# Where a graph kernel puts its running group states: scattered to each node's row as they finish, or stored densely and gathered by node at the end

## The reference

```python
w_m = (efeat @ W_msg + b_msg).reshape(E, in_f, -1)
w_a = (efeat @ W_attn + b_attn).reshape(E, in_f, -1)
h_src = feat[src][:, :, None]
e1 = w_m * h_src
e2 = w_a * h_src
seg_max = jax.ops.segment_max(e2, dst, num_segments=N)
ex = jnp.exp(e2 - seg_max[dst])
denom = jax.ops.segment_sum(ex, dst, num_segments=N)
attn = ex / denom[dst]
ft = jax.ops.segment_sum(e1 * attn, dst, num_segments=N)
return ft.sum(axis=1)
```

## Time and profile before

| | us |
|---|---|
| median of 3 runs | 6419.38 (6419.01 to 6424.5) |
| the profiled execution's time | 6420.29 |
| its span | 6418.6 |
| DVE busy in the span | 5261.2 (82%) |
| POOL busy | 4903.2 (76%) |
| PE busy | 4765.4 (74%) |
| ACT busy | 2628.9 (41%) |

### The profile page before, as it was taken

One profiled execution on the slowest core, in us unless ns is written; L12 is line 12 of the kernel. 1 busy time (PEld: TensorE's weight loads), 2 busy tenths in 40 slices (PEclk: granted clock), 3 DMA queues, 4 the chain that ended last, 5 costly groups with the idle time before them and its releaser, 6 DMA issues. The chain is left out here.

```text
span 6418.6 us, 70875 instructions
## 1 busy us (share of the span) xinstructions
PE 4765.4 (74%) x18115; PEld 2257.7 (35%) x18115; DVE 5261.2 (82%) x8583; ACT 2628.9 (41%) x4866; POOL 4903.2 (76%) x4618
## 2 busy tenths in 40 slices
PE   1277777777777777775888888888888888888881
PEld 1133333333333333342333333333333333333330
DVE  5366666666666666667999999999999999999996
ACT  1122222222222222213555555555555555555553
POOL 6688888888888888855777777777777777777772
PEclk6588888888889898897889899989989889889895
DMA  4122222222222222210111111111111111111102
GB/s 123 50 68 72 68 68 69 68 68 72 63 54 54 54 54 54 53 39 13 16 17 16 16 16 16 16 16 17 16 16 16 16 16 16 16 16 16 16 15 105
DMA packets 386589, 255.80 MB, mean 40 GB/s; under 512 B 243117, under 2 KB 334678, under 8 KB 386305
## 3 DMA queue, kind: packets, MB, share of 16 engines
q0 software_dynamic: 226240, 167.32, 12.5%
q1 hardware_dynamic: 160318, 88.15, 4.6%
HBM read 186.95 MB, written 141.36 MB: 51 GB/s over the span
## 5 line engine op out<-in xcount | busy, mean ns | idle before, releaser
L587 POOL DMA_INDIRECT bg<-btab,mt x1600 | 2109.2, 1318 | 489.6 <-issue 464.3
L697 PE MATMUL pagg<-ohh,stt 125*128 125x512 bf16 x4800 | 1847.0, 421 | 743.6 <-DVE ohh L627 743.6
L947 POOL DMA_INDIRECT xg<-x1tab,edge x1920 | 1917.2, 999 | 550.0 <-issue 549.7
L1029 PE MATMUL ps<-work,ident 128*128 128x512 f32 x3840 | 2006.4, 647 | 0.2 <-DVE work L1117 0.2
L698 PE MATMUL pagg<-ohh,stt 125*128 125x270 bf16 x4800 | 1454.7, 303 | 0.0
L1078 DVE TENSOR_TENSOR work<-pw,xg 128x1024 f32<-128x1024 f32 x960 | 1125.8, 1214 | 56.8 <-DMA xg<-x1tab,edge 25.8
L1029 PEld LDWEIGHTS ps<-work,ident 128*128 128x128 f32 x3840 | 817.5, 213 | 748.2 <-issue 656.1
L697 PEld LDWEIGHTS pagg<-ohh,stt 125*128 125x128 bf16 x4800 | 510.6, 106 | 1496.5 <-DVE ohh L627 822.0
L678 ACT COPY ohx<-ohl 125x1024 bf16<-125x1024 bf16 x200 | 208.8, 1044 | 1971.7 <-DVE ohl L617 1971.7
L610 DVE TENSOR_TENSOR bg<-bg,e 125x1024 f32<-125x1024 f32 x200 | 245.1, 1225 | 839.6 <-DMA bg<-btab,mt 839.6
L988 ACT ACTIVATE work<-work,mt 128x256 f32<-128x256 f32 x1920 | 793.1, 498 | 3.5 <-DVE work L1078 3.3
(11 more groups left out here) (232 smaller groups left out, 4247.6 us busy)
## 6 DMA issues: line engine op xcount, KB each, us to landing
xg<-x1tab,edge POOLq DMA_INDIRECT x1920, 2.4
bg<-btab,mt POOLq DMA_INDIRECT x1600, 3.5
rtab<-zrow SPq DMA_DIRECT2D x56, 384.0 KB, 3.9
tab<-rtab SPq DMA_DIRECT2D x7, 2048.0 KB, 8.4
etab<-joined SPq DMA_DIRECT2D x200, 66.4 KB
e<-in_edge_attr_dram SPq DMA_DIRECT2D x200, 62.5 KB
e<-in_edge_attr_dram SPq DMA_DIRECT2D x200, 31.2 KB
mt<-meta SPq DMA_DIRECT2D x240, 6.0 KB, 1.8
```

The costliest lines, as they stand in the source:

```text
L587: g.indirect_dma_start(bg[:, h, i, :], None, btab, bass.IndirectOffsetOnAxis(ap=mt[:, h, 0, i:i + 1], axis=0)).then_inc(gathered[h], 16)
L697: pe.matmul(pagg[:, 0, :], w, ohh[:, h, i, 0:CUT], start=False, stop=False, skip_group_check=True)
L947: g.indirect_dma_start(xg[:, b % 4, i, :], None, x1tab, bass.IndirectOffsetOnAxis(ap=edge[:, b, i, D:D + 1], axis=0)).then_inc(x_in[b % 4] ...
L1029: pe.matmul(ps[:, b % 2, :], ident[:, :], work[:, b % 4, i, :, :, :].rearrange("p i a o -> p (i a o)"), start=i == 0, stop=False)
```

## The change

- `rtab` is gone. Two dense tables take its place, `smax` (one row of 256 floats for each group) and `ssum` (512 floats), with two fixed rows behind them, `EMPTY` and `NEUTRAL`.
- In the second layer's loop SP stores every tile's whole `state` with two DMAs (128 x 2 KB and 128 x 1 KB), then loads the `mt` of 8 tiles on. POOL's scatter and its wait are gone. DVE's write into a state buffer waits for both stores of 8 tiles earlier.
- In setup DVE works out for each node the number of its last group (7 small operations); SP writes it to `lasttab` and reads it back into `lasti` (3 DMAs). `meta1` shrinks from 12 to 10 words a group.
- The 56 + 2 filling DMAs of the first layer are replaced by 4 of one row each.
- In the merge the tails are read from the last group of each partition by SP, the heads with two indirect gathers on POOL.
- At the end 56 indirect gathers on POOL (7 blocks x 8, each 128 rows of 2 KB) replace SP's 7 loads, and DVE takes over POOL's multiplication.

```diff
@@ setup, vector
+                v.memset(pado[:, :], EMPTY).then_inc(last_step, 1)
+                v.tensor_scalar(final, first[:, 1:], float(E), None, ALU.is_ge).then_inc(last_step, 1)
...
+                v.tensor_scalar(lasto[:, :], final, float(EMPTY), None, ALU.add).then_inc(last_step, 1)
@@ setup, sync
+                sp.wait_ge(last_step, 7)
+                sp.dma_start(lasttab[0:N].rearrange("(p t) -> p t", p=P), lasto[:, :]).then_inc(last_out, 16)
+                sp.dma_start(lasttab[N:NPAD].rearrange("(p t) -> p t", t=9), pado[:, :]).then_inc(last_out, 16)
+                sp.wait_ge(last_out, 32)
+                sp.dma_start(lasti[:, :, :], lasttab.rearrange("(b p l) -> p b l", p=128, l=LO)).then_inc(last_in, 16)
@@ first layer, sync
-                    sp.dma_start(view[:, bass.ds(t * 3 * C, 3 * C)], zrow[:, :]).then_inc(table_cleared, 16)
@@ second layer, sync
+                def store(n, q):
+                    sp.wait_ge(st_done, n + 1)
+                    sp.dma_start(ssum[0:GP * NT, :].rearrange("(p t) c -> p (t c)", p=GP)[:, bass.ds(n * 2 * C, 2 * C)],
+                                 state[:, q, C:3 * C]).then_inc(stored[q], 16)
+                    sp.dma_start(smax[0:GP * NT, :].rearrange("(p t) c -> p (t c)", p=GP)[:, bass.ds(n * C, C)],
+                                 state[:, q, 0:C]).then_inc(stored[q], 16)
...
-                        sp.wait_ge(scattered[q], 16 * (t + 1))
+                        store(U * t + q, q)
                         load(U * t + q + U, q)
@@ second layer, gpsimd
-                    if at := tile(t, q, -2):
-                        n, b, r = at
-                        g.wait_ge(st_done, n + 1)
-                        g.nop(nofuse=True)
-                        g.indirect_dma_start(rtab, bass.IndirectOffsetOnAxis(ap=mt[:, b, 1:2], axis=0),
-                                             state[:, b, :], None,
-                                             bounds_check=ROWS - 1, oob_is_err=False).then_inc(scattered[b], 16)
@@ second layer, vector
-                    wait(v, scattered[b], 16 * r)
+                    wait(v, stored[b], 32 * r)
@@ merge, gpsimd
+                at = bass.IndirectOffsetOnAxis(ap=hrow[:, 0:1], axis=0)
+                g.indirect_dma_start(ht[:, 0, 0:C], None, smax, at).then_inc(head_in, 16)
+                g.indirect_dma_start(ht[:, 0, C:3 * C], None, ssum, at).then_inc(head_in, 16)
@@ end, gpsimd
                 for b in range(NB):
-                    s = tab[:, b % 3, :, 0, :]
-                    g.wait_ge(guessed, b + 1)
-                    g.tensor_tensor(s, s, inv[:, b % 2, :, :], ALU.mult).then_inc(off_by, 1)
+                    if b >= 3:
+                        g.wait_ge(f_step, 4 * (b - 2))
+                    for l in range(LO):
+                        g.indirect_dma_start(tab[:, b % 3, l * D:(l + 1) * D, :, :].rearrange("p i a o -> p (i a o)"), None,
+                                             ssum,
+                                             bass.IndirectOffsetOnAxis(ap=lasti[:, b, l:l + 1], axis=0)).then_inc(row_in[b], 16)
@@ end, vector
                     v.tensor_tensor(t, t, inv[:, b % 2, :, :], ALU.mult).then_inc(f_step, 1)
-                    v.wait_ge(off_by, b + 1)
+                    v.tensor_tensor(s, s, inv[:, b % 2, :, :], ALU.mult).then_inc(f_step, 1)
```

More of the change, by code:

```diff
@@ L55 @@
 U = 8
-MW = 12
+MW = 10
 KS = 99
+EMPTY, NEUTRAL = GP * NT, GP * NT + 1
+ROWS = GP * NT + 2
+SKIP = ROWS
 assert GP * NT * J >= E + (J - 1) * N and NT % U == 0
@@ L117, in gnn @@
         ends = sb("ends", [GP, 8])
+        hrow = sb("hrow", [GP, 1], I32)
+        lasti = sb("lasti", [128, NB, LO], I32)
         consts_made = sem("consts_made")
@@ L337, in _ @@
                                             op0=ALU.mult, op1=ALU.add))
-                deg, num, run, has = (ngf[:, i, :] for i in range(4))
+                deg, num, run, has, final, lastg = (ngf[:, i, :] for i in range(6))
                 link(v.tensor_tensor(deg, first[:, 1:], first[:, 0:TN], ALU.subtract))
@@ L561, in _ @@
                 sp.wait_ge(rows_made, 4)
-                sp.dma_start(rtab[HEAD:HEAD + 128, :], hrow[:, :]).then_inc(table_cleared, 16)
-                sp.dma_start(rtab[TAIL:TAIL + 128, :], hrow[:, :]).then_inc(table_cleared, 16)
-                per = NPAD // 128
-                view = rtab[0:NPAD, :].rearrange("(p r) c -> p (r c)", p=128)
-                with sp.Fori(0, per) as t:
-                    next_pair(t)
-                    sp.dma_start(view[:, bass.ds(t * 3 * C, 3 * C)], zrow[:, :]).then_inc(table_cleared, 16)
-                with sp.Fori(per, NBLK // 2 - 1) as t:
+                for r in range(2):
+                    sp.dma_start(smax[EMPTY + r:EMPTY + r + 1, :], fixed[:, r, 0:C]).then_inc(table_cleared, 16)
+                    sp.dma_start(ssum[EMPTY + r:EMPTY + r + 1, :], fixed[:, r, C:3 * C]).then_inc(table_cleared, 16)
+                with sp.Fori(0, NBLK // 2 - 1) as t:
                     next_pair(t)
@@ L575, in _ @@
                     sp.wait_ge(join_out[h], 16 * (NBLK // 2 + 1))
-                sp.wait_ge(table_cleared, 16 * (per + 2))
+                sp.wait_ge(table_cleared, 64)
             @block.gpsimd
@@ L851, in gnn @@
             x_in = [sem(f"l1_x_in{q}") for q in range(4)]
-            scattered = [sem(f"l1_scattered{q}") for q in range(U)]
+            stored = [sem(f"l1_stored{q}") for q in range(U)]
             primed = sem("l1_primed")
@@ L910, in _ @@
                     for q in range(U):
-                        sp.wait_ge(scattered[q], 16 * (t + 1))
-                        sp.nop(nofuse=True)
+                        store(U * t + q, q)
                         load(U * t + q + U, q)
+                for q in range(U):
+                    store(NT - U + q, q)
+                for q in range(U):
+                    sp.wait_ge(stored[q], 32 * (NT // U))
             @block.gpsimd
@@ L955, in body @@
                                              bass.IndirectOffsetOnAxis(ap=mt[:, b, 0:1], axis=0)).then_inc(edge_in[b % 4], 16)
-                rounds(g, body, 5, 2)
-                for q in range(U):
-                    g.wait_ge(scattered[q], 16 * (NT // U))
+                rounds(g, body, 5, 0)
             @block.scalar
@@ L1102, in maxima @@
                     wait(v, corr_done, n)
-                    v.scalar_tensor_tensor(out=gap[:, :], in0=state[:, (b - 1) % U, 0:C], scalar=word(b, 2),
+                    v.scalar_tensor_tensor(out=gap[:, :], in0=state[:, (b - 1) % U, 0:C], scalar=word(b, 1),
                                            in1=state[:, b, 0:C], op0=ALU.add, op1=ALU.subtract).then_inc(gap_done, 1)
@@ L1215, in _ @@
                 v.tensor_tensor(rowf[:, 1:2], ends[:, 1:2], ends[:, 2:3], ALU.not_equal).then_inc(step, 1)
-                v.tensor_scalar(rowf[:, 2:4], ends[:, 0:2], -float(SKIP), None, ALU.add).then_inc(step, 1)
+                v.tensor_scalar(rowf[:, 2:3], ends[:, 3:4], -float(SKIP), None, ALU.add)
+                v.tensor_scalar(rowf[:, 3:4], iota_p[:, 1:2], -float(SKIP), None, ALU.add).then_inc(step, 1)
                 v.wait_ge(step, 5)
```

99 lines of the change are left out of this document (55 added, 44 removed).

## The result

The changed kernel takes 6465.16 us (4 runs, 6464.75 to 6469.23) against 6419.19 beside it (4 runs, 6416.78 to 6424.5): ratio 1.0072, 95% interval 1.0054 to 1.0089. It is slower, by 46 us (0.7%) where 113 were forecast. The profiled execution has a span of 6463.1, 44.5 more than the 6418.6 of before.

| stretch | before | after | difference | forecast |
|---|---|---|---|---|
| to the first maximum | 2968.5 | 2966.8 | -1.7 | -1 |
| loop, first to last maximum | 3293.1 | 3321.8 | +28.7 | +96 |
| last maximum to the first read of the table | 61.7 | 56.0 | -5.7 | +1 |
| first read to L1366 (L1336 before) | 83.8 | 107.0 | +23.2 | +17 |
| the layer norm behind it | 11.5 | 11.5 | 0 | 0 |

The account below looks back on a forecast made before the run. The prediction took the loop to be bound by DVE and POOL together, both full and coupled through PE. Loop +96, setup -1, merge +1 and end +17 gave +113 us, 6532 by the median; 8-in-10 range 6420 to 6575.

Parts of the forecast that it names:

- steps 1 and 2: Loop: without the scatter POOL needs 12.65 us a tile, DVE's wait for PE goes; POOL runs ahead until ACT's copy.
- Step 3, the place: Loop: POOL's two tensor operations move from under L1078 to under the last L1117, L1089 and L1090.
- Step 3, the price: Loop: collision priced by the second tile's 14.23 us, three stretched DVE operations, less 0.05 for the scatter: 14.18 a tile.
- The loop's term: Second layer's loop: 239 tiles at 14.18 us instead of 13.78, +96 us, with a range of +75 to +115.
- The single stretch: Rival, loop: only one DVE operation stretches, 13.73 us a tile, -12, with the end 6424; chance 0.10.
- The first rival: Loop: POOL's pair stays under L1078 or ahead of it, 13.51 us a tile, -64, total 6372; chance 0.16.
- The end: End of kernel: POOL's gathers replace SP's loads and DVE takes over POOL's multiplication; +17 us, between +10 and +26.
- nothing disturbs: End, lower case: DVE's blocks of 10.7 us run without POOL's gathers being held up, +10 us.
- a gather each: End, upper case: one gather gets through in each of three DVE operations, a block takes 13.5 us, +26.
- Between loop and end: Merge: two gathers of 1.28 us in place of two loads, +1 us.
- First layer, setup, stores: Outside the loop's collision: removing first-layer gathers is worth 0, setup -1 us, SP's stores cost 0.
- The full lock: Rival, loop: each of POOL's two operations costs DVE its whole 0.45 us, +62 more, 6594; chance 0.04.

Follow-up runs that it names:

- e4: Kernel after, with POOL's pair of tensor operations held until DVE's `gap` of the tile is done: 6470.9 us (one run).
- e1: Kernel after, with POOL's pair of tensor operations held until DVE's `carry_on` of that tile is done: 6412.5 us, ratio 0.9996 to the kernel before.
- e5: Kernel after, with 1/denominator and the first product of the end in PSUM, leaving DVE's tensor-tensor operations one SBUF input each: 6458.8 us.
- e3: Kernel after, with each tile's state stored twice, the second time into tables nobody reads: 6468.4 us (one run).
- e10: Kernel after, with POOL's pair held until `carry_on` and its order swapped, end operands in PSUM, and a wait making a gap in DVE's products: 6397.8 us.
- e6: Kernel after, with POOL's pair held until `carry_on` and the end's operands in PSUM: 6406.9 us.

## Why the prediction was right, and where it was wrong

- **What bounds the kernel, and steps 1 and 2**: right. PE's wait for the pair went (517.2 to 38.1 us), the edges' four take 4.61, POOL moved up until ACT's copy stopped it, in 230 tiles.
- **Step 3, the place**: right. The pair begins under the last product (0.02 us after its start) and goes on under L1115 and L1116, where the prediction had put it.
- **Step 3, the price**: this is the step that failed. "I price them by the tile that shows this collision: 14.23 us" took three stretched operations from the earlier trace rows. After the change the pair stretches two: 13.51 + 2 x 0.22 = 13.95 by the prediction's own figures, 13.90 measured. The tile taken for the price was one in which POOL ran straight from a gather into L933 (0.01 us between them). Step 2 had POOL wait for ACT ahead of that operation in each tile, and in the traces a pair that comes after a wait never stretches the operation that already runs. So the price of step 3 came from a state that step 2 had ruled out. The kernel before has no pair that comes after a wait with such an operation running, so its trace could not tell the price; e4 and the kernel after could. The third stretch was 0.23 x 239 = 55 us of the miss, the difference of 13.95 and 13.90 the other 12. The tile had no scatter either (the first starts at 3001.15 us), so the 0.05 that the prediction took off for it was not there to be taken off; this went the right way by luck. The loop's term was +96 and is +28.7, 67 us less. The total missed by 67 too, because the end (6 us more than forecast) and the stretch ahead of it (7 less) cancel, which is luck.
- **The single stretch**, the rival at 6424, was 41 us too low, where the forecast was 67 too high. The measured time lies between the two, where the prediction had put no case, though its wide range took it in.
- **The first rival** (POOL stays clear) did not come by itself. e1 made it by hand and found its tile, 13.51, but not its mean: 13.68, for PE's clock.
- **The end**: +23.2 against +17, inside 10 to 26. The middle between "nothing disturbs" and "a gather each" was too kind. The upper case is what the later blocks show: three of eight gathers are held, and the block is 13.0 us for its 13.5, since the held ones start every 2.2 us or so and the others every 1.25. DVE began 17.9 us after the first gather, against 18.5. e5 shows that DVE's second SBUF input is the cause.
- **Between loop and end**: -5.7 against +1. The last scatter before the barrier was not in the sum; the wait behind it fell by 8.0 us.
- **First layer, setup, stores**: 0, -1 and 0 were right to 1 us; e3 shows it for the stores.
- **The full lock**: the Trainium skill, SBUF — State Buffer, "Who interferes with whom", would have POOL's operation exclude DVE for its whole length. In the loop each stretched operation loses 0.23 us (0.91 for 0.68), against a POOL operation of 0.42 to 0.45 alone, so the rows disagree. For gathers the rule comes nearer: one waits for DVE's operation, or for a run of six (4.08 us), though DVE's own operations keep their length.

What no step had: the kernel before takes 6415 to 6420 us in three of the six sets of runs and 6792 to 6803 in the three others, on other chips. The kernel after takes 6465 to 6469 on chips of the first kind, and took 6477 on the one of the second kind where it ran. There the change is worth 4.7%.

Of the versions, e10 at 6397.8 and e6 at 6406.9 are the shortest. Both ran only where the kernel before takes 6800, 6% above them. They are 0.1 to 0.3% below the 6415 to 6420 of the other chips, but that compares different chips and is not a measured ratio. e1 is level with the kernel before (0.9996) on the same chip.

## What to carry to other kernels

When an engine is freed, ask not how much it saves but where its remaining work will slide to, and price the collision there by the number of operations of the other engine that begin under it. Take the price from a tile in which the freed engine arrives as it will after the change: here it would come after a wait, and the tile used had it come without one. A wait can be worth having: one that keeps two SBUF-to-SBUF operations on POOL under DVE's operations from PSUM took off some 50 us. Before trusting a base time, run it on more than one chip.

## What was not expected of the hardware

- Two operations on POOL cost DVE 0.23 us for each of two of its operations, whether these take 0.68 or lie in a run of four (2.87 for 2.45), and nothing where DVE reads PSUM (4.61 for four edge operations). A third is stretched, the one that already runs, only where POOL came to them without waiting: in 345 of 354 cases, against none of 1867.
- An indirect DMA of POOL that starts 0.40 to 0.55 us behind the start of a gap-free run of DVE operations with two SBUF inputs can be shut out until the run's end, 4.08 us for 0.95, or pass in 1.05, and with the same start to 0.02 us both happen.
- PE's signal to ACT, 0.04 us as a rule, came 2 to 6.5 us late in 109 of 240 tiles on one chip, and came late 73 times, with no record that explains it, on another. In the steady loop this was seen only in kernels with the scatter; its cause is open.
